# A Perceiver block's first cross-attention: the context's fp16 remainders made by GpSimd instead of VectorE

## The chip, the cores and the metric

The kernel runs on one core of a Trainium2 chip. The metric is the device time of one execution in microseconds (us); lower is better. The engines are named as the profile names them: PE is TensorE's matmul unit (PEld its weight load), DVE is VectorE, ACT is ScalarE, POOL is GpSimd and SP the engine that issues the DMAs.

## The reference

A block of six residual steps works on 128 latent rows of 256 channels. The first step, in which the change lies, is a cross-attention of 16 heads over a context of 12544 rows:

```python
xn = _layernorm(x, ln_gamma, ln_beta)
q = (xn @ w_q).reshape(B, SQ, NUM_HEADS, DIM_HEAD)      # 128 queries, 16 heads of 64
kv = context @ w_kv                                     # context 12544 x 256, w_kv 256 x 2048
k, v = jnp.split(kv, 2, axis=-1)
scores = jnp.einsum('bqhd,bkhd->bhqk', q * SCALE, k)
attn = jax.nn.softmax(scores, axis=-1)
out = jnp.einsum('bhqk,bkhd->bqhd', attn, v).reshape(B, SQ, INNER)
return (out @ w_out + b_out) * jnp.tanh(gate[0])
```

Then follow a causal attention, a feed-forward with quantised weights, a second cross-attention over the same context, a selective scan and a mixture of experts. All arithmetic is fp32 in the reference.

## The kernel before

`first_cross_attention` cuts the context into 14 chunks of 896 rows (`NCH = 14`, `CH = 896`, chunk `c`) and walks in each through the 16 heads `h`; one head of one chunk is a step, `n = 16 * c + h`, 224 steps in all. Every engine has its own program, written out by hand in Python loops over `n`; each executes its program strictly in order, and the engines are coupled by counting semaphores alone.

fp32 operands are split into two fp16 parts, a rounded one and a remainder, and three fp16 products stand in for one fp32 product. For the context this split is made once per chunk, one chunk ahead, in four pieces `k` of 128 x 448: ScalarE writes the rounded part `c_hi` (`c_high`, at its steps h = 5 to 8), VectorE the remainder `c_lo` = `c_raw` * `c_scale` - `c_hi` (`c_low`, one instruction per piece, at its steps h = 6 to 9). `c_raw` is the loaded fp32 chunk; it has one buffer, and `c_hi` and `c_lo` have two (`par`).

The parts of a step, by engine:

- TensorE, step n: `turn_max(n + 1)` (L793, by which the start of a step is seen), the key products of unit U = n + 6 (`k_wait(U)`, then `k_part`, L771, six products), `first_pass(n + 2)`, `lay_max(n + 1)` (L798), `weigh(n - 1)`, `second_pass(n + 1)`, and at 14 of the 16 steps (not at h = 0 and 8) six value products (`v_project`, L743). A unit U holds the keys of two heads for half a chunk, so the units 16(c+1) and 16(c+1)+1, made at h = 10 and h = 11, are the first that read the next chunk.
- ScalarE, step n: value rounding, `p_high(n)`, `m_row(n + 1)`, `k_copy(n + 6)` into `k_raw`, `exponent(n + 1)`, then `c_high` where it is due, and at every fourth step the `decay` of the running maximum.
- VectorE, step n: `new_max(n + 1)` (L601), `v_low` (or `c_low` of piece 3 at h = 9), `tiles_max(n + 2)` (L592), every fourth step `flush`, `p_low(n)` (`pT_lo`, L606), then `c_low` of pieces 0 to 2 at h = 6 to 8.
- GpSimd, step n: at h % 4 = 3 the scaling of the accumulator (`acc`, L421), which waits for ScalarE's `decay` of the same step; `k_split(n + 6)`, a cast `k_top` (L404) and a subtraction `k_rest` (L406) that split `k_raw`; at h % 4 = 2 `group_max` (L391 to L396).
- SP issues the DMAs that place `k_top` and `k_rest` in `k_st`, and at h = 11 the load of the next but one chunk into `c_raw`.

The waits of TensorE for the remainders are these (`c_lo_ready` counts finished pieces, four a chunk):

```python
if u < 2:                                   # k_wait(U), u = U % 16: first two units of a chunk
    pe.wait_ge(c_lo_ready, 4 * c + 2 + 2 * u)
if half == 0:                               # v_project, steps h = 9 to 15
    pe.wait_ge(c_lo_ready, 4 * c + (2 if tile < 3 else 4))
```

So pieces 0 and 1 of the next chunk are wanted at the end of TensorE's step h = 9, and all four at its step h = 11. ScalarE's `k_copy` waits until `k_rest` of two units earlier is done, since `k_raw` has two buffers.

Of the kernel before, what the change touches and what calls it, by code (L numbers as in the profile page):

```python
# [5 lines left out]
ALU = mybir.AluOpType  # L6
# [14 lines left out]
NCH = SK // CH  # L21
# [27 lines left out]
def at_least(engine, sem, value):  # L49

    if isinstance(value, int) and value <= 0:
        return
    engine.wait_ge(sem, value)
# [98 lines left out]
def first_cross_attention(nc, ctx, a, sb, sem, x, z, y, zT, ident, st, stats, rows, cols, gate, ps,  # L152
# [11 lines left out]
    with ExitStack() as own:  # L164
        def t(name, shape, dt=F32):
            return sb(name, shape, dt, own)
# [15 lines left out]
        c_raw = t("c_raw", [P, DC, CH])  # L182
        c_hi, c_lo = t("c_hi", [P, 2, DC, CH], F16), t("c_lo", [P, 2, DC, CH], F16)
        c_abs, c_scale = t("c_abs", [P, 2, 4]), t("c_scale", [P, 2, DC])
# [21 lines left out]
        def tf_half(w, j):  # L206
            return w[TERNARY[j // 2]][:, j % 2 * INNER:(j % 2 + 1) * INNER]
# [20 lines left out]
        c_hi_ready, c_lo_ready = sem("c_hi_ready"), sem("c_lo_ready")  # L228
# [41 lines left out]
        def v_at(n):  # L270

            c, h = n // H0, n % H0
            if 1 <= h <= TILES:
                return c * 14 + 6 + h, c, 1, h - 1
            if h >= 9 and c + 1 < NCH:
                return c * 14 + 5 + h, c + 1, 0, h - 9
            return None
# [10 lines left out]
        def raw_part(k):  # L288
            return (slice(None), k % 2, slice(k // 2 * HCH, (k // 2 + 1) * HCH))

        def c_part(par, k):
            return (slice(None), par, k % 2, slice(k // 2 * HCH, (k // 2 + 1) * HCH))

        with nc.Block() as block:
# [56 lines left out]
            def _(pool):  # L351
                link = plink.on(pool)
# [23 lines left out]
                def unscale(c):  # L376
                    par = c % 2
                    pool.wait_ge(un_ready, c + 1)
                    nc.gpsimd.tensor_scalar(v_unscale[:, par:par + 1], un[:, par:par + 1], 1.0 / W_TOP, None, ALU.mult).then_inc(unscale_ready, 1)
                    nc.gpsimd.tensor_scalar(esc[:, par:par + 1], un[:, par:par + 1], q_un[:, 0:1], DH ** -0.5 / (W_TOP * K_DOWN), ALU.mult, ALU.mult).then_inc(unscale_ready, 1)  # L380
                    pool.wait_ge(unscale_ready, 2 * c + 2)
                    pool.wait_ge(c_scale_ready, c + 1)
                    link(nc.gpsimd.tensor_scalar(m_per[:, par:par + 1], un_inv[:, par:par + 1], q_scale[:, 0:1], W_TOP * K_DOWN * DH ** 0.5, ALU.mult,
                                                 ALU.mult))

                def group_max(c, g):

                    par, hs = c % 2, slice(4 * g, 4 * g + 4)
                    at_least(pool, decay_ready, c * 4 + g - 3)
                    pool.wait_ge(m_ready, c * H0 + 4 * g + 4)  # L390
                    link(nc.gpsimd.tensor_scalar(run_max[:, par, hs], m_col[:, par, hs], esc[:, par:par + 1], None, ALU.mult))  # L391
                    nc.gpsimd.tensor_tensor(drop[:, hs], run_max[:, 1 - par, hs], run_max[:, par, hs], ALU.subtract).then_inc(drop_ready, 1)
                    f = c * 4 + g + 2
                    if 4 <= f < NCH * 4:
                        par, hs = f // 4 % 2, slice(4 * (f % 4), 4 * (f % 4) + 4)
                        nc.gpsimd.tensor_scalar(m_floor[:, hs], run_max[:, 1 - par, hs], m_per[:, par:par + 1], None, ALU.mult).then_inc(floor_ready, 1)  # L396

                def k_split(U):
                    i, b = U - K_AHEAD, U % 2

                    pool.wait_ge(k_raw_ready, i + 1)
                    if i >= 2:
                        pool.wait_ge(k_placed[b], k_turn(U - 2))
                    nc.gpsimd.tensor_copy(k_top[:, b, :], k_raw[:, b, :]).then_inc(k_top_ready, 1)  # L404
                    pool.wait_ge(k_top_ready, i + 1)
                    nc.gpsimd.tensor_tensor(k_rest[:, b, :], k_raw[:, b, :], k_top[:, b, :], ALU.subtract).then_inc(k_rest_ready, 1)  # L406
# [5 lines left out]
                for n in range(NT):  # L412
                    c, h = n // H0, n % H0
                    if h % 4 == 3:
                        g = h // 4
                        f = c * 4 + g

                        pool.wait_ge(decay_ready, f + 1)
                        at_least(pool, flushed, 2 * (f - 3))
                        grp = acc[:, 4 * g:4 * g + 4, :]  # L420
                        nc.gpsimd.tensor_tensor(grp, grp, decay[:, 4 * g:4 * g + 4].unsqueeze(2).to_broadcast([P, 4, DH + 1]),  # L421
                                                ALU.mult).then_inc(acc_scaled, 1)
                    if n + K_AHEAD < NT:
                        k_split(n + K_AHEAD)
                    if h == 5 and c + 1 < NCH:
                        unscale(c + 1)
                    if h % 4 == 2:
                        group_max(c, h // 4)

            @block.scalar  # L430
            def _(act):
# [124 lines left out]
            def _(v):  # L556
                link = vlink.on(v)
# [13 lines left out]
                def c_low(c, k):  # L571
                    par = c % 2
                    v.wait_ge(c_hi_ready, 4 * c + k + 1)
                    nc.vector.scalar_tensor_tensor(out=c_lo[c_part(par, k)], in0=c_raw[raw_part(k)], scalar=c_scale[:, par, k % 2:k % 2 + 1],
                                                   in1=c_hi[c_part(par, k)], op0=ALU.mult, op1=ALU.subtract).then_inc(c_lo_ready, 1)
# [19 lines left out]
                def new_max(n):  # L595
                    c, h, i = n // H0, n % H0, n % 2
                    m = m_col[:, c % 2, h:h + 1]
                    v.wait_ge(max_turned, n + 1)
                    if c > 0 and h % 4 == 0:
                        v.wait_ge(floor_ready, c * 4 + h // 4 - 3)  # L600
                    nc.vector.tensor_scalar(turned[:, i, :], s_turned(n), 1.0, -BIG if c == 0 else m_floor[:, h:h + 1], ALU.mult, ALU.max,  # L601
                                            accum_out=m).then_inc(m_ready, 1)
# [77 lines left out]
                for n in range(NT):  # L680
                    c, h = n // H0, n % H0
                    if n + 1 < NT:
                        new_max(n + 1)
                    if n and v_at(n - 1):
                        v_low(*v_at(n - 1))
                    elif c + 1 < NCH:
                        if h == 1:
                            absmax(c + 1, 2)
                        if h == 9:
                            c_low(c + 1, 3)  # L690
                    if n + 2 < NT:
                        tiles_max(n + 2)
                    if h % 4 == 1 and n > 1:
                        flush(n // 4 - 1)
                    p_low(n)
                    if h == 15 and c + 2 < NCH:
                        absmax(c + 2, 0)
                    if c + 1 < NCH:
                        if h in (0, 3):
                            absmax(c + 1, (1, 2, 0, 3)[h])  # L700
                        if h == 4:
                            scale(c + 1)
                        if 6 <= h <= 8:
                            c_low(c + 1, h - 6)
                    if c == 1 and h == 4:
                        v.wait_ge(tf_total, 1)
                        link(nc.vector.tensor_reduce(tf_mean[:, :], s_total.rearrange("p (k b) -> p k b", b=2), AX.X, ALU.add))
                        link(nc.vector.tensor_scalar(tf_mean[:, :], tf_mean[:, :], 1.0 / (D * INNER), 1e-5, ALU.mult, ALU.max))
                        nc.vector.reciprocal(tf_inv[:, :], tf_mean[:, :]).then_inc(tf_mean_ready, 1)
                    if 2 <= c < 8 and h == 13:  # L710
                        j = c - 2
                        v.wait_ge(tf_scaled, 2 * j + 2)
                        link(nc.vector.tensor_scalar(tf_half(tf_raw, j), tf_half(tf_raw, j), ROUND, 1.0, ALU.subtract, ALU.min))
                    if 2 <= c < 8 and h == 15:
                        j = c - 2
                        nc.vector.tensor_scalar(tf_half(tf_wq, j), tf_half(tf_raw, j), -1.0, None, ALU.max).then_inc(tf_quantised, 1)
# [1136 lines left out]
```

## Time and profile before

| | before |
| --- | --- |
| median of 3 runs | 1372.73 us |
| lowest, highest | 1368.29, 1372.86 us |
| profiled execution, its own time | 1368.9 us |
| its span, first to last instruction | 1367.2 us |
| PE busy | 1157.3 us (85%) |
| DVE busy | 1075.5 us (79%) |
| ACT busy | 857.6 us (63%) |
| POOL busy | 625.3 us (46%) |

The profile is one execution, followed by the hardware profiler. The busy shares are averages over all six residual steps; the first one fills the span from about 50 to about 970 us, and only it contains the instructions of the change. PE's spans are modelled, so its distance from full use is better read from the starts of its steps than from its busy share.

### The profile page before, as it was taken

To read this page: it belongs to the slowest core of one execution; us is meant where nothing else is said; L and a number is where in the kernel's file an instruction comes from. 1 tells how busy PE (TensorE), PEld (TensorE's weight loads), DVE (VectorE), ACT (ScalarE), POOL (GpSimd) and SP (SyncE) were. 2 spreads that over 40 slices of the span, in tenths; PEclk is the share of its full clock that TensorE was granted. 3 is DMA by queue.
4 is the path that set the end of the run, shared out by engine and by line. 5 is a ranking of instruction groups with operands and counts; after the bars stand their busy time and mean duration, and the time that the engine had idled before them with its cause. 6 is when DMAs were issued, how large, how long until landed. Compare 5 with 4: busy or idle time off the path is not lost. (4 is left out here: it accounts for less than half of the span.)

```text
span 1367.2 us, 31601 instructions
## 1 busy us (share of the span) xinstructions
PE 1157.3 (85%) x12091; PEld 794.4 (58%) x12091; DVE 1075.5 (79%) x1757; ACT 857.6 (63%) x1453; POOL 625.3 (46%) x734
## 2 busy tenths in 40 slices
PE   3699999999999999999999999999539895135598
PEld 1366666666666666666666666666415584012397
DVE  7678989898989899999898998988445414999522
ACT  2489888888888888888888888888310231550010
POOL 5056666565656666656666566665000000556000
PEclk9999999999999999999999999999858997576699
DMA  5154343434343434344443434334356370500165
GB/s 198 57 134 110 84 118 92 113 88 111 86 113 86 109 82 113 87 111 93 113 116 89 113 83 117 85 91 97 138 183 202 107 228 2 215 0 1 69 233 186
DMA packets 137137, 152.21 MB, mean 111 GB/s; under 512 B 17617, under 2 KB 125457, under 8 KB 136737
## 3 DMA queue, kind: packets, MB, share of 16 engines
q1 hardware_dynamic: 136176, 147.12, 39.7%
q10 hardware_dynamic: 816, 3.15, 0.6%
q8 instruction: 93, 1.52, 0.5%
q14 instruction: 52, 0.42, 0.1%
HBM read 74.34 MB, written 0.16 MB: 54 GB/s over the span
## 5 line engine op out<-in xcount | busy, mean ns | idle before, releaser
L406 POOL TENSOR_TENSOR k_rest<-k_raw,k_top 128x448 f16<-128x448 f32 x218 | 316.3, 1451 | 17.6
L476 ACT ACTIVATE p_exp<-ps,ln_k,esc 128x896 f32<-128x896 f32 x224 | 246.1, 1099 | 70.3 <-PE ps L807 65.5
L606 DVE TENSOR_TENSOR pT_lo<-p_exp,pT_hi 128x896 f16<-128x896 f32 x224 | 271.4, 1212 | 2.3 <-ACT pT_hi L494 2.3
L592 DVE TENSOR_REDUCE tile_max<-ps 128x128 f16<-128x896 f32 x224 | 243.3, 1086 | 33.4 <-PE ps L784 33.1
L404 POOL CAST k_top<-k_raw 128x448 f16<-128x448 f32 x218 | 143.2, 657 | 223.0 <-ACT k_raw L489 180.8
L494 ACT ACTIVATE pT_hi<-p_exp 128x896 f16<-128x896 f32 x224 | 211.3, 943 | 0.6
L587 DVE TENSOR_TENSOR v_lo<-ps,v_hi 128x512 f16<-128x512 f32 x196 | 135.1, 689 | 49.8 <-ACT v_hi L468 46.0
L821 PE MATMUL ps<-v_hi,pT_hi 128*128 128x65 f16 x1568 | 164.1, 193 | 2.5 <-DVE pT_lo L606 2.5
L822 PE MATMUL ps<-v_lo,pT_hi 128*128 128x64 f16 x1568 | 164.2, 193 | 0.0
L823 PE MATMUL ps<-v_hi,pT_lo 128*128 128x65 f16 x1568 | 163.8, 193 | 0.0
L771 PE MATMUL ps<-c_hi,wk_hi 128*128 128x448 f16 x448 | 158.3, 353 | 3.7 <-DVE k_st L658 3.6
L771 PE MATMUL ps<-c_hi,wk_lo 128*128 128x448 f16 x448 | 158.6, 354 | 0.0
L771 PE MATMUL ps<-c_lo,wk_hi 128*128 128x448 f16 x448 | 158.4, 354 | 0.0
L743 PE MATMUL ps<-wv_lo,c_hi 128*128 128x512 f16 x392 | 149.1, 380 | 0.0
L743 PE MATMUL ps<-wv_hi,c_lo 128*128 128x512 f16 x392 | 149.1, 380 | 0.0
L743 PE MATMUL ps<-wv_hi,c_hi 128*128 128x512 f16 x392 | 149.1, 380 | 0.0
L821 PEld LDWEIGHTS ps<-v_hi,pT_hi 128*128 128x128 f16 x1568 | 144.9, 98 | 2.8 <-DVE pT_lo L606 2.8
L823 PEld LDWEIGHTS ps<-v_hi,pT_lo 128*128 128x128 f16 x1568 | 142.9, 97 | 0.0
L822 PEld LDWEIGHTS ps<-v_lo,pT_hi 128*128 128x128 f16 x1568 | 142.8, 97 | 0.0
L784 PEld LDWEIGHTS ps<-q_hi,k_st 128*128 128x128 f16 x1568 | 105.8, 98 | 49.1 <-ACT p_exp L476 5.5
L468 ACT ACTIVATE v_hi<-ps 128x512 f16<-128x512 f32 x196 | 116.4, 594 | 26.3 <-PE ps L743 22.7
L784 PE MATMUL ps<-q_hi,k_st 128*128 128x128 f16 x1568 | 124.1, 219 | 7.8 <-ACT p_exp L476 3.0
(330 smaller groups left out, 2120.4 us busy)
## 6 DMA issues: line engine op xcount, KB each, us to landing
k_st<-k_top SPq DMA_DIRECT2D x436, 112.0 KB, 2.3
k_st<-k_rest SPq DMA_DIRECT2D x436, 56.0 KB, 2.0
c_raw<-in_ctxT SPq DMA_DIRECT2D x14, 896.0 KB, 5.9
xa_ct<-in_ctxT SPq DMA_DIRECT2D x14, 896.0 KB, 4.7
xa_cn<-in_ctx SPq DMA_DIRECT2D x14, 896.0 KB, 5.1
me_w<-in_me_w SPq DMA_DIRECT2D x8, 1536.0 KB, 7.8
me_w<-in_me_w SPq DMA_DIRECT2D x8, 768.0 KB, 4.8
ss_b_all<-ss_bc SPq DMA_DIRECT2D x1, 2048.0 KB, 6.7
```

The source lines that it names most:

```text
L404: nc.gpsimd.tensor_copy(k_top[:, b, :], k_raw[:, b, :]).then_inc(k_top_ready, 1)
L406: nc.gpsimd.tensor_tensor(k_rest[:, b, :], k_raw[:, b, :], k_top[:, b, :], ALU.subtract).then_inc(k_rest_ready, 1)
L476: nc.scalar.activation(p_exp[:, n % 2, :], s_scores[n % 2], ACT.Exp, bias=ln_k[:, 0:1], scale=esc[:, n // H0 % 2:n // H0 % 2 + 1]).then_in ...
L494: nc.scalar.activation(pT_hi[:, n % 2, :, :].rearrange("p t s -> p (t s)"), p_exp[:, n % 2, :], ACT.Copy).then_inc(pT_hi_ready, 1)
L592: nc.vector.tensor_reduce(tile_max[:, n % 2, :], s_scores[n % 2].rearrange("p (t s) -> p s t", s=S), AX.X, ALU.max).then_inc(tile_max_done, 1)
L606: nc.vector.tensor_tensor(pT_lo[:, n % 2, :, :].rearrange("p t s -> p (t s)"), p_exp[:, n % 2, :], pT_hi[:, n % 2, :, :].rearrange("p t s ...
L743: mm = nc.tensor.matmul(v_bank(vn), lhs, rhs, start=(k == 0), stop=(k == 5))
L771: mm = nc.tensor.matmul(k_bank(U), lhs, rhs, start=(k == 0), stop=(k == 5))
L784: mm = nc.tensor.matmul(s_scores[i][:, tile * S:(tile + 1) * S], k_st[:, n // 2 % 4, i, 0, tile * P:(tile + 1) * P], q_hi[:, h, :], start= ...
L821: nc.tensor.matmul(to, ph, v_hi[:, tile, h, 0:DH + 1], start=(tile == 0), stop=False)
L822: nc.tensor.matmul(to[:, 0:DH], ph, v_lo[:, tile, h, 0:DH], start=False, stop=False)
L823: mm = nc.tensor.matmul(to, pl, v_hi[:, tile, h, 0:DH + 1], start=False, stop=(tile == TILES - 1))
```

## The change

VectorE's `c_low` goes from its steps h = 6 to 9 (it stays for chunk 0, before the loop). GpSimd does the same pieces at its steps h = 6 to 9, behind `k_split` and `group_max` of the step. It has no single instruction for it there: it first scales a piece of `c_raw` in place and then subtracts `c_hi`, with a wait on its own semaphore between (`link`). TensorE's, ScalarE's and SP's programs are unchanged.

```diff
@@ gpsimd, at the end of step n
                     if h % 4 == 2:
                         group_max(c, h // 4)
+                    if 6 <= h <= 9 and c + 1 < NCH:
+                        k, par = h - 6, (c + 1) % 2
+                        pool.wait_ge(c_hi_ready, 4 * (c + 1) + k + 1)
+                        link(nc.gpsimd.tensor_scalar(c_raw[raw_part(k)], c_raw[raw_part(k)], c_scale[:, par, k % 2:k % 2 + 1], 1.0, ALU.mult, ALU.mult))
+                        nc.gpsimd.tensor_tensor(c_lo[c_part(par, k)], c_raw[raw_part(k)], c_hi[c_part(par, k)], ALU.subtract).then_inc(c_lo_ready, 1)
@@ vector, step n
                     elif c + 1 < NCH:
                         if h == 1:
                             absmax(c + 1, 2)
-                        if h == 9:
-                            c_low(c + 1, 3)
...
                         if h == 4:
                             scale(c + 1)
-                        if 6 <= h <= 8:
-                            c_low(c + 1, h - 6)
```

On GpSimd, from the accumulator's scaling (`acc`) of step h = 7 to the maximum (`run_max`) of h = 10, the order was this: four splits of the keys in a row (h = 7 to 10).

```order
L421 TENSOR_TENSOR acc<-acc,decay 128x260
L404 CAST k_top<-k_raw 128x448
L406 TENSOR_TENSOR k_rest<-k_raw,k_top 128x448
L404 CAST k_top<-k_raw 128x448
L406 TENSOR_TENSOR k_rest<-k_raw,k_top 128x448
L404 CAST k_top<-k_raw 128x448
L406 TENSOR_TENSOR k_rest<-k_raw,k_top 128x448
L404 CAST k_top<-k_raw 128x448
L406 TENSOR_TENSOR k_rest<-k_raw,k_top 128x448
L391 TENSOR_SCALAR run_max<-m_col,esc 128x4
```

In the changed kernel, in the same stretch from the row behind `acc` on, GpSimd's order is this (piece 0 stands ahead of `acc`, behind the `group_max` of h = 6).

```order
L404 CAST k_top<-k_raw 128x448
L406 TENSOR_TENSOR k_rest<-k_raw,k_top 128x448
L432 TENSOR_SCALAR c_raw<-c_raw,c_scale 128x448
L433 TENSOR_TENSOR c_lo<-c_raw,c_hi 128x448
L404 CAST k_top<-k_raw 128x448
L406 TENSOR_TENSOR k_rest<-k_raw,k_top 128x448
L432 TENSOR_SCALAR c_raw<-c_raw,c_scale 128x448
L433 TENSOR_TENSOR c_lo<-c_raw,c_hi 128x448
L404 CAST k_top<-k_raw 128x448
L406 TENSOR_TENSOR k_rest<-k_raw,k_top 128x448
L432 TENSOR_SCALAR c_raw<-c_raw,c_scale 128x448
L433 TENSOR_TENSOR c_lo<-c_raw,c_hi 128x448
```

Between `acc` and the last remainder of a chunk now stand three splits of the keys and three pairs of the new instructions, where the remainders took no place in this queue before.

On VectorE, from `pT_lo` of step h = 7 to `tile_max` of step h = 9, the order was this.

```order
L606 TENSOR_TENSOR pT_lo<-p_exp,pT_hi 128x896
L574 SCALAR_TENSOR_TENSOR c_lo<-c_raw,c_scale,c_hi 128x448
L601 TENSOR_SCALAR turned,m_col<-ps 128x128
L587 TENSOR_TENSOR v_lo<-ps,v_hi 128x8x64
L592 TENSOR_REDUCE tile_max<-ps 128x128
L606 TENSOR_TENSOR pT_lo<-p_exp,pT_hi 128x896
L574 SCALAR_TENSOR_TENSOR c_lo<-c_raw,c_scale,c_hi 128x448
L601 TENSOR_SCALAR turned,m_col<-ps 128x128
L574 SCALAR_TENSOR_TENSOR c_lo<-c_raw,c_scale,c_hi 128x448
L592 TENSOR_REDUCE tile_max<-ps 128x128
```

In the changed kernel the same stretch of VectorE's queue is this (its lines lie five further down).

```order
L611 TENSOR_TENSOR pT_lo<-p_exp,pT_hi 128x896
L606 TENSOR_SCALAR turned,m_col<-ps 128x128
L592 TENSOR_TENSOR v_lo<-ps,v_hi 128x8x64
L597 TENSOR_REDUCE tile_max<-ps 128x128
L611 TENSOR_TENSOR pT_lo<-p_exp,pT_hi 128x896
L606 TENSOR_SCALAR turned,m_col<-ps 128x128
L597 TENSOR_REDUCE tile_max<-ps 128x128
```

Nothing but `c_lo` is gone, so `turned` (`new_max`) stands directly behind `pT_lo`.

## Rows read from the trace of the kernel before

**Rows 1.** Busy time of PE, PEld, DVE, ACT, POOL; clock, DMA share, GB/s.

```profile
100.00:950.00 850.00, 826.16 (x10211) 561.72 (x10210) 768.56 (x1277) 715.06 (x1145) 523.76 (x665) 1.00 0.42 100
```

**Rows 2.** Timeline of PE, chunk 9, h = 7 to 12: start, duration, [idle before].

```profile
686.19 0.22 PE L793 MATMUL ps<-ident,tile_max 128*128 128x128 f16 x1
...
688.10 0.23 PE L798 MATMUL ps<-ident,m_col 128*128 128x128 f16 x1 [0.16 <-DVE turned L601]
...
690.47 0.22 PE L793 MATMUL ps<-ident,tile_max 128*128 128x128 f16 x1
...
693.40 0.23 PE L793 MATMUL ps<-ident,tile_max 128*128 128x128 f16 x1
...
695.63 0.23 PE L798 MATMUL ps<-ident,m_col 128*128 128x128 f16 x1 [0.47 <-DVE turned L601]
...
698.28 0.22 PE L793 MATMUL ps<-ident,tile_max 128*128 128x128 f16 x1
...
702.30 0.22 PE L793 MATMUL ps<-ident,tile_max 128*128 128x128 f16 x1
702.36 0.35 PE L771 MATMUL ps<-c_hi,wk_hi 128*128 128x448 f16 x1
...
706.25 0.22 PE L793 MATMUL ps<-ident,tile_max 128*128 128x128 f16 x1
```

**Rows 3.** Timeline of DVE, the same chunk: `pT_lo` and `c_lo`.

```profile
686.31 1.45 DVE L574 SCALAR_TENSOR_TENSOR c_lo<-c_raw,c_scale,c_hi 128x448 f16<-128x448 f32 x1
...
689.56 1.07 DVE L606 TENSOR_TENSOR pT_lo<-p_exp,pT_hi 128x896 f16<-128x896 f32 x1
690.56 0.67 DVE L574 SCALAR_TENSOR_TENSOR c_lo<-c_raw,c_scale,c_hi 128x448 f16<-128x448 f32 x1
...
693.26 1.14 DVE L606 TENSOR_TENSOR pT_lo<-p_exp,pT_hi 128x896 f16<-128x896 f32 x1
694.33 0.97 DVE L574 SCALAR_TENSOR_TENSOR c_lo<-c_raw,c_scale,c_hi 128x448 f16<-128x448 f32 x1
...
695.49 1.18 DVE L574 SCALAR_TENSOR_TENSOR c_lo<-c_raw,c_scale,c_hi 128x448 f16<-128x448 f32 x1
...
698.06 1.35 DVE L606 TENSOR_TENSOR pT_lo<-p_exp,pT_hi 128x896 f16<-128x896 f32 x1
...
701.21 1.24 DVE L606 TENSOR_TENSOR pT_lo<-p_exp,pT_hi 128x896 f16<-128x896 f32 x1
```

**Rows 4.** Timeline of POOL, the same chunk.

```profile
688.20 0.30 POOL L396 TENSOR_SCALAR m_floor<-run_max,m_per 128x4 f32<-128x4 f32 x1
691.21 0.62 POOL L421 TENSOR_TENSOR acc<-acc,decay 128x260 f32<-128x260 f32 x1 [2.71 <-ACT decay L534]
691.78 0.56 POOL L404 CAST k_top<-k_raw 128x448 f16<-128x448 f32 x1
692.42 1.04 POOL L406 TENSOR_TENSOR k_rest<-k_raw,k_top 128x448 f16<-128x448 f32 x1
693.40 1.42 POOL L404 CAST k_top<-k_raw 128x448 f16<-128x448 f32 x1
694.90 1.29 POOL L406 TENSOR_TENSOR k_rest<-k_raw,k_top 128x448 f16<-128x448 f32 x1
696.79 0.56 POOL L404 CAST k_top<-k_raw 128x448 f16<-128x448 f32 x1 [0.60 <-ACT k_raw L489]
...
701.58 1.76 POOL L406 TENSOR_TENSOR k_rest<-k_raw,k_top 128x448 f16<-128x448 f32 x1
```

**Rows 5.** Groups by line and shape: count | busy us, mean ns | idle.

```profile
L574 DVE SCALAR_TENSOR_TENSOR c_lo<-c_raw,c_scale,c_hi 128x448 f16<-128x448 f32 x51 | 54.3, 1064 | 0.0
...
L380 POOL TENSOR_SCALAR esc<-un,q_un 128x1 f32<-128x1 f32 x14 | 3.7, 267 | 1.3
...
L374 POOL CAST ident<-ident 128x128 f16<-128x128 f32 x1 | 0.3, 291 | 0.1
```

**Rows 6.** Timeline of ACT, the same chunk: `pT_hi` of h = 11.

```profile
703.00 0.94 ACT L494 ACTIVATE pT_hi<-p_exp 128x896 f16<-128x896 f32 x1
```

## The prediction

> **What bounds the kernel now.** I read first the busy time of the engines in the stretch from 100 to 950 us, which is inside the first cross-attention [rows 1]. PE is busy for 826.16 of 850 us at full clock, DVE for 768.56, ACT for 715.06, POOL for 523.76. So TensorE sets the pace, VectorE runs close behind it, and GpSimd seems to have room: 38% of its time is free.
>
> Then I read the starts of TensorE's steps in one chunk [rows 2]. A step starts at L793. The step h = 11, from 702.30 to 706.25, lasts 3.95 us and shows no wait, so I take 3.95 as TensorE's own time for a step with value products. The steps around VectorE's `c_low` are h = 7: 690.47 - 686.19 = 4.28; h = 8 (no value products): 693.40 - 690.47 = 2.93; h = 9: 698.28 - 693.40 = 4.88; h = 10: 702.30 - 698.28 = 4.02. Over 3.95 that is 0.33 at h = 7, 0.93 at h = 9 and 0.07 at h = 10; h = 8 can't be compared so; I give it 0.2. The bracketed waits of 0.16 and 0.47 us name `turned`, the instruction that stands behind `c_lo` on VectorE [rows 2, 3]. VectorE's remainders thus cost TensorE at most about 1.5 us a chunk, and that is the most the relief can bring: 13 x 1.5 = 20 us.
>
> Last I read GpSimd's own timeline in that chunk, because an average of 38% free says nothing about one queue at one place. Behind its `group_max` (688.20 + 0.30) it idles 2.71 us until `decay` of h = 7 is there and `acc` starts, at 691.21 [rows 4]. From there it has 11.15 us until TensorE starts the key products of h = 11 at 702.36 [rows 2], which in the changed kernel want all four pieces of `c_lo`.
>
> **How GpSimd and VectorE share time.** The cast `k_top` takes 0.56 us when nothing disturbs it, but 1.42 at 693.40, beside the `pT_lo` of 693.26 [rows 3, 4]: 0.86 more. The subtraction `k_rest` takes 1.04 at 692.42, but 1.76 at 701.58, beside the `pT_lo` of 701.21: 0.72 more. In reverse, `pT_lo` of 698.06 lasts 1.35 beside `k_rest`'s tail, against 1.07 at 689.56, and `c_lo` lasts 0.67 alone and up to 1.45. So the two engines exclude each other in these instructions, and each `pT_lo` takes about 0.86 us out of a busy GpSimd queue. (The Trainium skill, "SBUF — State Buffer", section "SBUF: two separate sides", calls the pair of ports an exclusive lock that the loser waits for; the trace's 0.86 agrees.)
>
> **The change part by part.**
>
> VectorE loses 4 instructions per chunk, 13 chunks, of 1064 ns on average [rows 5]. By the above that frees at most 1.5 us of TensorE's time a chunk.
>
> GpSimd gains 4 pairs a chunk. The subtraction has the shape and types of `k_rest`: from 692.42 to the next start at 693.40, 0.98 us. The in-place scaling (fp32 out, two multiplies, one by a value per partition) is in no row. From below it is bounded by the cast of the same size, 0.56; from above by the two-input subtraction, 1.04. Between them I build it from small rows: a scaling with two scalars on one column costs 0.267, and the cast of 128 columns 0.291 against 0.56 for 448, which is 0.84 ns a column; 0.267 + 447 x 0.00084 = 0.64 us [rows 4, 5]. With the 0.08 us that a wait on its own semaphore costs (691.78 + 0.56 to 692.42), the pair is 0.64 + 0.08 + 0.98 = 1.70 us. A split of the keys is 0.64 + 0.98 = 1.62.
>
> The Trainium skill speaks more strongly against the move: "GPSIMD Engine Reference", section 3, has a two-input elementwise operation 1.96 times as long on GpSimd as on VectorE. From c_lo's undisturbed 0.67 that would be a subtraction of 1.31 instead of 1.04 us; three of them would add 0.8 us a chunk, 11 us in all. The row of `k_rest` is the same operation on the same shape, so I keep 1.04.
>
> Piece 0 is free: it stands in the 2.71 us of idle before `acc`. It needs 1.70, and one `pT_lo` (689.56) falls into it, 0.86, in sum 2.56.
>
> From the start of `acc` to the end of piece 3 the queue now holds: `acc` 0.57, three splits 3 x 1.62 = 4.86, three pairs 3 x 1.70 = 5.10, and three `pT_lo` that cut in (those of h = 8, 9, 10; that of h = 11 can't start before its `pT_hi` ends at 703.94 [rows 6], and comes as late as TensorE does) 3 x 0.86 = 2.58. The sum is 13.11 us, and 0.1 for the signal. There is no gap to win back: `k_raw` is ready earlier than GpSimd comes to it (at 696.79 it had still waited 0.60 for it). TensorE would be ready after 11.15. **So it waits 13.2 - 11.15 = 2.1 us at `k_wait` of step h = 11, in each of 13 chunks: 27 us.** Behind that wait are `first_pass`, `lay_max`, `weigh` and `second_pass`, so ScalarE and VectorE stand still with it, and the whole pipeline shifts.
>
> What is given back: the relief of h = 8 to 10 is lost, since it only brings TensorE to the same wait sooner. Relief ahead of `acc` counts, because it starts the chain earlier: of h = 7's 0.33, the 0.16 that was a wait plus a little, say 0.2. And VectorE enters h = 11 without arrears, another 0.25. In sum 0.45 x 13 = 6 us.
>
> Other consumers have room. Pieces 0 and 1 are ready at 691.21 + 0.57 + 1.62 + 1.70 + 0.86 = 695.96; TensorE wants them in the last microsecond of h = 9, from about 697. `k_rest` of h = 9 ends near 701.8, ScalarE's copy that needs it free is that of h = 11. The placed keys are wanted three and more steps later. SP's load of `c_raw` stands behind `k_rest` of h = 11 in both kernels.
>
> The sum: 27 - 6 = +21 us. On the profiled execution's 1368.9 that is 1390; on the median of 1372.73, which is 3.8 above it, 1394. I say **1392 us**.
>
> **The rivals.**
>
> *A, the forecast: GpSimd's queue is late for h = 11, by 1 to 3 us.* 1380 to 1405. Chance 0.68.
>
> *B, GpSimd is much later.* If the scaling costs the upper bound, 1.04, each pair is 0.40 longer and the wait 3 x 0.40 = 1.2 longer: 13 x 1.2 = 16 us more, about 1408. If each `pT_lo` takes its full 1.07, 0.6 us a chunk more, 8 us. For it: no row has fp32 written by GpSimd at this width. Against it: the small scalings cost no more than the small cast. Chance 0.16.
>
> *C, faster: the remainders are in time.* This needs the chain to fit in 11.15 us: 10.53 of GpSimd's own work, so each `pT_lo` may take no more than 0.2 us from it. Then TensorE gets back its excess up to the moment when piece 3 is there, 702.36 - 701.9 = 0.5, with 0.45 from above about 0.9 us a chunk, 12 us: 1360. For it: the casts of 691.78 and 696.79 run undisturbed in 0.56 [rows 4], as if room could be found between VectorE's instructions. Against it: in a queue without idle each `pT_lo` must hold up one instruction or the next. Chance 0.07.
>
> *D, no change.* The wait is 0.3 to 0.7 us, as large as what is given back. This needs a `pT_lo` to cost about 0.4. 1366 to 1379. Chance 0.09.
>
> **How the numbers follow.** A measurement of this kernel tells 0.5%, 7 us, from no change. Slower by more: A and B, 0.84; within: D, 0.09; faster: C, 0.07. The range has the lower end from the short values (scaling 0.56, `pT_lo` 0.72 each: wait 1.4, less 0.45: 12 us, and somewhat more given back), and the upper from B: 1377 to 1410.
>
> **What would show it.** After the change TensorE's L771 at h = 11 should show a wait of about 2 us for GpSimd's `c_lo`, 13 times, some 25 us in all, and be the longest wait of TensorE in the stretch. VectorE's busy time in it should fall by about 50 us, with longer `pT_lo` at h = 7 to 10. GpSimd should run without idle from `acc` of h = 7 to piece 3, 13.1 us. The scaling should read 0.64 us undisturbed. The prediction is wrong if that wait is absent (then C or D), or if ScalarE waits for `k_rest` (then more is late than I see).

## The result: slower by 2.4%

The changed kernel takes 1403.79 us (median of 4 runs, 1402.34 to 1408.41), the kernel before 1372.8 us (4 runs). The ratio is 1.024, 95% interval 1.0207 to 1.0272: 31 us more. The forecast was 1392, with a range from 1377 to 1410: the direction and the place were right, the size was over a third too small (19 us forecast, 31 measured).

The page of the changed kernel, its first part and the groups that changed (lines lie one to five further down than before):

```profile
span 1400.6 us, 31653 instructions
...
PE 1164.9 (83%) x12091; PEld 803.1 (57%) x12091; DVE 1044.3 (75%) x1705; ACT 858.7 (61%) x1453; POOL 711.4 (51%) x838
...
L597 DVE TENSOR_REDUCE tile_max<-ps 128x128 f16<-128x896 f32 x224 | 243.9, 1089 | 78.9 <-PE ps L785 78.6
...
L772 PE MATMUL ps<-c_hi,wk_hi 128*128 128x448 f16 x448 | 159.9, 357 | 34.3 <-POOL c_lo L433 30.7
```

VectorE's busy time fell from 1075.5 to 1044.3 us: `c_lo` takes 55.7 us less, `pT_lo` 14.7 us more (from 271.4 to 286.1). What VectorE gained it spends waiting for TensorE (78.9 us of idle ahead of `tile_max`, where it was 33.4). The view of who waited for whom, for PE, from 100 to 970 us (waiter, releaser: us in total, times, longest):

```profile
PE ps L772 <- POOL c_lo L433: 30.7, 13, 2.5
PE ps L808 <- ACT q_low L488: 6.8, 20, 1.4
PE ps L799 <- DVE turned L606: 5.8, 18, 0.5
```

Thirteen waits, one for each chunk that has a successor, all at the key products and all for GpSimd's remainder. Twelve of them last 2.47 or 2.48 us; the one in the first chunk lasts 1.03. The wait for `turned` is down to 5.8 us in 18 times. In the kernel before, the same view had this, the part around `c_lo` included:

```profile
PE ps L798 <- DVE turned L601: 14.7, 44, 1.0
```

GpSimd's timeline in chunk 9 answers to [rows 4]:

```profile
707.50 0.30 POOL L396 TENSOR_SCALAR m_floor<-run_max,m_per 128x4 f32<-128x4 f32 x1
707.78 0.64 POOL L432 TENSOR_SCALAR c_raw<-c_raw,c_scale 128x448 f32<-128x448 f32 x1
708.50 1.04 POOL L433 TENSOR_TENSOR c_lo<-c_raw,c_hi 128x448 f16<-128x448 f32 x1
710.56 0.62 POOL L421 TENSOR_TENSOR acc<-acc,decay 128x260 f32<-128x260 f32 x1 [1.01 <-ACT decay L539]
711.12 0.56 POOL L404 CAST k_top<-k_raw 128x448 f16<-128x448 f32 x1
711.76 1.04 POOL L406 TENSOR_TENSOR k_rest<-k_raw,k_top 128x448 f16<-128x448 f32 x1
712.78 1.48 POOL L432 TENSOR_SCALAR c_raw<-c_raw,c_scale 128x448 f32<-128x448 f32 x1
714.34 1.04 POOL L433 TENSOR_TENSOR c_lo<-c_raw,c_hi 128x448 f16<-128x448 f32 x1
...
719.51 0.56 POOL L404 CAST k_top<-k_raw 128x448 f16<-128x448 f32 x1
720.14 1.84 POOL L406 TENSOR_TENSOR k_rest<-k_raw,k_top 128x448 f16<-128x448 f32 x1
721.97 0.64 POOL L432 TENSOR_SCALAR c_raw<-c_raw,c_scale 128x448 f32<-128x448 f32 x1
722.68 1.03 POOL L433 TENSOR_TENSOR c_lo<-c_raw,c_hi 128x448 f16<-128x448 f32 x1
```

And PE's, at its step h = 11 of the same chunk and the start of the next step:

```profile
721.17 0.22 PE L794 MATMUL ps<-ident,tile_max 128*128 128x128 f16 x1
...
723.86 0.35 PE L772 MATMUL ps<-c_hi,wk_hi 128*128 128x448 f16 x1 [2.47 <-POOL c_lo L433]
...
727.75 0.22 PE L794 MATMUL ps<-ident,tile_max 128*128 128x128 f16 x1
```

Piece 3 is finished at 723.71, 13.15 us behind the start of `acc`; between the two GpSimd has no bracket of idle. The scaling lasts 0.64 us undisturbed, and 1.48 at 712.78, 0.84 more, where VectorE is in this `pT_lo`:

```profile
712.61 1.14 DVE L611 TENSOR_TENSOR pT_lo<-p_exp,pT_hi 128x896 f16<-128x896 f32 x1
```

TensorE reaches step h = 11 at 721.17, 10.61 us behind `acc` and not 11.09, because the relief of h = 9 and 10 did come, and then it waits. Its step lasts 727.75 - 721.17 = 6.58 us instead of 3.95.

Something in the same place was not foreseen. In chunk 6 the products behind the wait are slow:

```profile
517.87 0.22 PE L794 MATMUL ps<-ident,tile_max 128*128 128x128 f16 x1
...
520.56 0.39 PE L772 MATMUL ps<-c_hi,wk_hi 128*128 128x448 f16 x1 [2.48 <-POOL c_lo L433]
520.75 0.57 PE L772 MATMUL ps<-c_lo,wk_hi 128*128 128x448 f16 x1
521.12 0.58 PE L772 MATMUL ps<-c_hi,wk_lo 128*128 128x448 f16 x1
...
526.10 0.22 PE L794 MATMUL ps<-ident,tile_max 128*128 128x128 f16 x1
```

and the granted clock of the stretch behind the wait, from 520.6 to 524.0 us, and of the next one is (PE, PEld, DVE, ACT, POOL busy; clock, DMA share, GB/s):

```profile
520.60:524.00 3.40, 3.40 (x24) 2.19 (x25) 0.40 (x1) 0.27 (x2) 2.10 (x5) 0.52 0.29 66
524.80:528.00 3.20, 3.20 (x33) 1.95 (x31) 2.06 (x5) 2.70 (x5) 1.64 (x3) 1.00 0.07 18
```

0.52 is the lower of the two levels, 1.2 instead of 2.4 GHz. This step lasts 526.10 - 517.87 = 8.23 us, 1.65 more than that of chunk 9. It happened behind 7 of the 12 waits of 2.47 us and not behind the one of 1.03 (the L772 products start 0.37 us apart there and 0.19 elsewhere); the seven steps last 8.05 to 8.24 us, 11.3 us in all over the 6.58 of the others; in the kernel before, the clock stands at 1.00 over the whole stretch [rows 1].

### The profile page after: what moved, and what is told of

Its sections match the earlier page's. It is cut to its first block and busy times, and to the rows that moved or that the text cites. A ratio compares the mean times of both kernels' runs of the same rounds, so it can differ in the third digit from the quotient of the medians.

```text
span 1400.6 us, 31653 instructions
## 1 busy us (share of the span) xinstructions
PE 1164.9 (83%) x12091; PEld 803.1 (57%) x12091; DVE 1044.3 (75%) x1705; ACT 858.7 (61%) x1453; POOL 711.4 (51%) x838
## 5 line engine op out<-in xcount | busy, mean ns | idle before, releaser
L406 POOL TENSOR_TENSOR k_rest<-k_raw,k_top 128x448 f16<-128x448 f32 x218 | 312.8, 1435 | 17.6
L597 DVE TENSOR_REDUCE tile_max<-ps 128x128 f16<-128x896 f32 x224 | 243.9, 1089 | 78.9 <-PE ps L785 78.6
L611 DVE TENSOR_TENSOR pT_lo<-p_exp,pT_hi 128x896 f16<-128x896 f32 x224 | 286.1, 1277 | 2.5 <-ACT pT_hi L499 2.5
L404 POOL CAST k_top<-k_raw 128x448 f16<-128x448 f32 x218 | 130.6, 599 | 182.3 <-ACT k_raw L494 142.1
L772 PE MATMUL ps<-c_hi,wk_hi 128*128 128x448 f16 x448 | 159.9, 357 | 34.3 <-POOL c_lo L433 30.7
L822 PE MATMUL ps<-v_hi,pT_hi 128*128 128x65 f16 x1568 | 167.3, 194 | 2.5 <-DVE pT_lo L611 2.5
L823 PE MATMUL ps<-v_lo,pT_hi 128*128 128x64 f16 x1568 | 167.3, 194 | 0.0
L824 PE MATMUL ps<-v_hi,pT_lo 128*128 128x65 f16 x1568 | 166.7, 194 | 0.0
L772 PE MATMUL ps<-c_hi,wk_lo 128*128 128x448 f16 x448 | 160.8, 359 | 0.0
L772 PE MATMUL ps<-c_lo,wk_hi 128*128 128x448 f16 x448 | 160.7, 359 | 0.0
L808 PE MATMUL ps<-q_low,k_st 128*128 128x128 f16 x1568 | 125.3, 220 | 9.3 <-ACT q_low L488 9.1
```

What stands on the lines that cost most here:

```text
L597: nc.vector.tensor_reduce(tile_max[:, n % 2, :], s_scores[n % 2].rearrange("p (t s) -> p s t", s=S), AX.X, ALU.max).then_inc(tile_max_done, 1)
L611: nc.vector.tensor_tensor(pT_lo[:, n % 2, :, :].rearrange("p t s -> p (t s)"), p_exp[:, n % 2, :], pT_hi[:, n % 2, :, :].rearrange("p t s ...
L772: mm = nc.tensor.matmul(k_bank(U), lhs, rhs, start=(k == 0), stop=(k == 5))
L822: nc.tensor.matmul(to, ph, v_hi[:, tile, h, 0:DH + 1], start=(tile == 0), stop=False)
L823: nc.tensor.matmul(to[:, 0:DH], ph, v_lo[:, tile, h, 0:DH], start=False, stop=False)
L824: mm = nc.tensor.matmul(to, pl, v_hi[:, tile, h, 0:DH + 1], start=False, stop=(tile == TILES - 1))
```

## The experiments

Eight kernels ran, in two groups of four; their times stand against the kernel before in the same group (1372.82 us, then 1371.01 us).

**Does the clock account for the rest?** `warm` is the changed kernel; TensorE does ten products that nobody reads, into the bank that the real ones then overwrite, before it waits.

```diff
+                    if u == 1 and c > 0:
+                        for k in range(10):
+                            nc.tensor.matmul(k_bank(U), wk_hi[:, 0, 0:P], c_hi[:, 1 - c % 2, 0, 0:HCH], start=True, stop=True)
                     if u < 2:
                         pe.wait_ge(c_lo_ready, 4 * c + 2 + 2 * u)
```

> TensorE does ten throwaway key products (128x448, overwritten by the real ones) at h = 11 before it waits for the remainders, so it works through most of the 2.5 us wait. Clock theory: 7 of the 13 waits of the changed kernel are followed by 3.4 us at the lower clock, 1.6 us lost each, 11 us in all; with TensorE kept busy the clock stays up, L772 products behind the wait take 0.35 us and never 0.57, and the time falls from 1404 to about 1393. Rival: the extra behind the wait is the pipeline's latency when it resumes; then the time stays at 1404 though the clock stays up.

It takes 1391.46 us (1390.24 to 1393.25), 1.0142 of the kernel before (1.0117 to 1.0167), and 12.3 us less than the changed kernel, by doing more work. PE at h = 11 of chunk 9, where the ten products fill the wait and nothing behind them is slow:

```profile
715.57 0.22 PE L797 MATMUL ps<-ident,tile_max 128*128 128x128 f16 x1
715.63 2.05 PE L764 MATMUL ps<-c_hi,wk_hi 128*128 128x448 f16 x10
718.17 0.36 PE L775 MATMUL ps<-c_hi,wk_hi 128*128 128x448 f16 x1 [0.49 <-POOL c_lo L433]
718.37 0.35 PE L775 MATMUL ps<-c_lo,wk_hi 128*128 128x448 f16 x1
...
722.07 0.22 PE L797 MATMUL ps<-ident,tile_max 128*128 128x128 f16 x1
```

The step lasts 6.50 us here and 6.50 or 6.51 in eleven other chunks; piece 3 is ready as late as before (13.16 us behind `acc`), and the granted clock shows 1.00 from 100 to 970 us. Only in the first chunk, where the wait was short, do the ten products make the step longer (5.84 instead of 5.14 us). The rival is refuted: the time did not stay at 1404, and a step behind a wait of 2.47 us at full clock was 6.58, hardly more than here. So about 12 of the 31 us are the clock (11.3 by the seven steps), and 1391.46 - 1372.82 = 18.6 us are the wait less the relief.

**Does GpSimd's order set the wait?** `swap` lets the pair of a step stand ahead of its key split.

```diff
+                    if 6 <= h <= 9 and c + 1 < NCH:
+                        ... the pair of piece h - 6
                     if n + K_AHEAD < NT:
                         k_split(n + K_AHEAD)
                     if h == 5 and c + 1 < NCH:
                         unscale(c + 1)
                     if h % 4 == 2:
                         group_max(c, h // 4)
-                    if 6 <= h <= 9 and c + 1 < NCH:
-                        ... the pair of piece h - 6
```

> GpSimd does the pair of a step ahead of the key split and not behind it. Queue theory: only two splits (2 x 1.62) and three pairs (3 x 1.70) stand between acc and piece 3, so it is ready 10.6 to 11.5 us behind the start of acc instead of 13.3, TensorE comes at 10.6, waits 0 to 0.9 us, and the clock stays up; 1361 to 1374 us. Rival: GpSimd is simply overloaded and the splits, now late, hold up ScalarE's k_copy or the placing; then the time stays near 1400 with a wait of ScalarE for k_rest.

1377.71 us, ratio 1.0034 (1.0018 to 1.005): 26 us are won back, but 5 stay; the time is 4 us above the upper end expected. Piece 3 is ready 10.8 to 11.6 us behind `acc`, as expected. The waits of PE and ACT from 100 to 950 us:

```profile
PE ps L808 <- ACT q_low L488: 9.7, 27, 1.4
PE ps L772 <- POOL c_lo L427: 6.3, 8, 0.8
```

```profile
ACT decay L539 <- POOL drop L392: 10.0, 14, 1.4
ACT k_raw L494 <- POOL k_rest L406: 3.0, 9, 0.4
```

TensorE's wait for the remainders is down from 30.7 to 6.3 us, and the clock stays up. What is new is that ScalarE waits for GpSimd: 10.0 us for `drop`, in 12 of the 14 cases that of h = 6, ahead of which the pair and the split of its step now stand, and 3.0 for `k_rest`, as the rival said in its milder half. In neither of the two orders tried do the four pairs fit into GpSimd's queue at these steps without making someone wait.

**Which term of the sum?** `no_scale` leaves out the scaling of `c_raw` on GpSimd, so that the subtraction works on unscaled values and the remainders are wrong numbers.

```diff
-                        link(nc.gpsimd.tensor_scalar(c_raw[raw_part(k)], c_raw[raw_part(k)], c_scale[:, par, k % 2:k % 2 + 1], 1.0, ALU.mult, ALU.mult))
                         nc.gpsimd.tensor_tensor(c_lo[c_part(par, k)], c_raw[raw_part(k)], c_hi[c_part(par, k)], ALU.subtract).then_inc(c_lo_ready, 1)
```

> Leaves out the in-place scaling on GpSimd in the changed kernel (the context's remainders are then wrong numbers). Queue theory: three scalings with their waits, 3 x 0.72 = 2.2 us, go from the chain behind acc, piece 3 is ready at about 11.1 instead of 13.3, TensorE comes at 10.6 and waits 0.5 us, too short for the clock: 1372.8 - 0.9 x 13 + 0.5 x 13 = 1367 to 1370 us. Rival: the lock and not the sum of instructions decides; then a part of the 31 us stays, 1385 or more.

1363.46 us, ratio 0.9933 (0.9907 to 0.9958). PE has no wait for `c_lo` left at all. This is 4 us below the expected 1367 to 1370: piece 3 is ready 10.15 us behind `acc` and not 11.1, since with the shorter queue one `pT_lo` fewer falls into it. What then shows is the relief of VectorE alone: a period of a chunk is 0.9 us shorter, as expected, and 40 us lie between this and the changed kernel. It does not decide against the lock: the 3.0 us by which the chain is shorter are three scalings with their waits, 2.16, and one `pT_lo`, 0.84.

**And the ports?** `short_before` and `short_after` are the two kernels with a `pT_lo` of 128 of its 896 columns from the third step on; the other columns keep old values, so part of the attention's low product is stale.

```diff
-                    nc.vector.tensor_tensor(pT_lo[:, n % 2, :, :]..., p_exp[:, n % 2, :], pT_hi[:, n % 2, :, :]..., ALU.subtract)
+                    full = n < 2
+                    nc.vector.tensor_tensor(pT_lo[:, n % 2, 0:TILES if full else 1, :]..., p_exp[:, n % 2, 0:CH if full else S],
+                                            pT_hi[:, n % 2, 0:TILES if full else 1, :]..., ALU.subtract)
```

> The kernel before with pT_lo computed for 128 of its 896 columns from the third step on (the rest stays stale). It is the base for short_after. VectorE gets 0.8 us a step shorter, so TensorE's arrears to it fall: 1340 to 1365 us; k_rest should take 1.04 to 1.2 us on average instead of 1.45.

> The changed kernel with the same short pT_lo. Lock theory: each pT_lo now takes 0.1 to 0.2 us from GpSimd and not 0.86, so piece 3 is ready 10.9 to 11.2 us behind acc, TensorE waits 0.3 to 0.6 us without a clock loss: 0 to 8 us above short_before. Rival, GpSimd's own instructions make it late whatever VectorE does: piece 3 stays at 13 us and the difference is 20 to 31 us as in the full pair.

1349.6 us (1348.57 to 1350.94) and 1350.23 us (1349.01 to 1350.93): no difference that these runs can tell, where the full pair differs by 31 us. `k_rest` takes 1075 ns on average in `short_before`, where it took 1451 with the full `pT_lo`, as expected. GpSimd in `short_after`, chunk 9, from `acc` on:

```profile
677.11 0.62 POOL L421 TENSOR_TENSOR acc<-acc,decay 128x260 f32<-128x260 f32 x1 [1.72 <-ACT decay L539]
677.67 0.56 POOL L404 CAST k_top<-k_raw 128x448 f16<-128x448 f32 x1
678.31 1.04 POOL L406 TENSOR_TENSOR k_rest<-k_raw,k_top 128x448 f16<-128x448 f32 x1
679.33 0.67 POOL L432 TENSOR_SCALAR c_raw<-c_raw,c_scale 128x448 f32<-128x448 f32 x1
...
686.83 1.04 POOL L433 TENSOR_TENSOR c_lo<-c_raw,c_hi 128x448 f16<-128x448 f32 x1
```

Piece 3 is ready 687.87 - 677.11 = 10.76 us behind `acc`, against 13.15: the same instructions, 2.4 us shorter, which is 0.8 for each of three `pT_lo`. The lock theory stands. The rival, GpSimd's own instructions alone, would have left it at 13. There is no gain to be seen either: in `short_before` TensorE's steps h = 7 and 10 are already down to 3.95 us, so the move has nothing left to relieve.

**What is the relief worth, and what does it take?** Three kernels give GpSimd a part of the pieces. The finished pieces are counted by one semaphore, and TensorE takes a count of two for pieces 0 and 1; so an engine waits for the other's earlier piece where the count would otherwise be wrong.

```diff
 g02, GpSimd, behind group_max
+                    if h in (6, 8) and c + 1 < NCH:
+                        ... the pair of piece h - 6, behind a wait for c_lo_ready >= 4 * (c + 1) + h - 6
 g02, VectorE
-                        if 6 <= h <= 8:
-                            c_low(c + 1, h - 6)
+                        if h == 7:
+                            v.wait_ge(c_lo_ready, 4 * (c + 1) + 1)
+                            c_low(c + 1, 1)
                         if h == 9:
+                            v.wait_ge(c_lo_ready, 4 * (c + 1) + 2)
                             c_low(c + 1, 3)
```

> GpSimd does pieces 0 and 2, VectorE 1 and 3. Queue theory: piece 2 is ready 7.2 us behind the start of acc, TensorE never waits for it; VectorE's relief at h = 7 (0.34 us a chunk) and part of that at h = 9 (0.2 to 0.4) stay: 1363 to 1368 us, faster than both kernels. Rival: the relief of VectorE is worth nothing, 1373.

`g0` does piece 0 on GpSimd and the other three on VectorE.

```diff
+                    if h == 6 and c + 1 < NCH:
+                        ... the pair of piece 0 on GpSimd; c_low of 1, 2 and 3 stays at h = 7, 8 and 9
```

> GpSimd does piece 0 alone, in the 2.7 us that it idles before acc. Queue theory: nothing on GpSimd is late; the gain is that of h = 7, 0.34 us x 13 = 4 us: 1368 us. Rival: the lock against pT_lo of h = 7 (1.83 us instead of 1.08) eats it: 1373.

`g03` does pieces 0 (h = 6) and 3 (h = 8) on GpSimd, 1 and 2 on VectorE.

```diff
+                    if h in (6, 8) and c + 1 < NCH:
+                        ... the pair of piece 0 or 3 on GpSimd; c_low of 1 and 2 stays at h = 7 and 8
```

> GpSimd does pieces 0 and 3 (at h = 6 and h = 8), VectorE 1 and 2; no remainder stands before tile_max of h = 9, where flush already stands on VectorE. Queue theory: ready 7 to 8 us behind acc, no wait; the whole excess of h = 9 is gone if it came from piece 3 on VectorE: 1360 to 1364. Rival: piece 2 on VectorE at h = 8 delays turned as before (0.47 us), so the time is that of the split into 0 and 2 or above: 1364 to 1370.

| kernel | on GpSimd | us, median | ratio to before (95%) |
| --- | --- | --- | --- |
| g0 | 0 | 1373.3 | 0.9999 (0.9985 to 1.0013) |
| g03 | 0, 3 | 1368.59 | 0.9981 (0.9965 to 0.9997) |
| g02 | 0, 2 | 1363.92 | 0.9918 (0.9893 to 0.9943) |
| changed kernel | 0, 1, 2, 3 | 1403.79 | 1.024 (1.0207 to 1.0272) |

`g02` beats both kernels. `g0` missed: the 4 us of h = 7 were expected and nothing came. Where each gains and loses is seen from TensorE's steps in chunk 9, in us from one start of a step to the next:

| kernel | h = 7 | h = 8 | h = 9 | h = 10 | sum |
| --- | --- | --- | --- | --- | --- |
| before | 4.28 | 2.93 | 4.88 | 4.02 | 16.11 |
| g0 | 3.95 | 3.19 | 4.99 | 4.02 | 16.15 |
| g03 | 3.95 | 3.18 | 4.76 | 3.95 | 15.84 |
| g02 | 3.94 | 3.19 | 4.23 | 3.95 | 15.31 |
| no_scale | 3.94 | 2.94 | 4.46 | 3.96 | 15.30 |
| changed kernel | 3.95 | 2.93 | 4.47 | 3.95 | 15.30 |

`g0` does gain at h = 7 and loses it at h = 8 and 9. Its own rival is the reason. GpSimd's pair and VectorE's queue in `g0`, chunk 9:

```profile
692.37 1.03 POOL L433 TENSOR_TENSOR c_lo<-c_raw,c_hi 128x448 f16<-128x448 f32 x1
694.41 1.01 POOL L421 TENSOR_TENSOR acc<-acc,decay 128x260 f32<-128x260 f32 x1 [1.01 <-ACT decay L539]
```

```profile
692.52 1.83 DVE L611 TENSOR_TENSOR pT_lo<-p_exp,pT_hi 128x896 f16<-128x896 f32 x1
694.27 0.67 DVE L579 SCALAR_TENSOR_TENSOR c_lo<-c_raw,c_scale,c_hi 128x448 f16<-128x448 f32 x1
694.87 0.34 DVE L606 TENSOR_SCALAR_CACHE_REDUCE turned<-ps,m_floor 128x128 f16<-128x128 f32 x1
```

`pT_lo` waits for GpSimd's subtraction (1.83 us instead of 1.07), piece 1 and `turned` come that much later, and the pieces 2 and 3 behind them pass it on. `g02` suffers the same at h = 7 (its h = 8 is as long), but with piece 2 gone VectorE is level again by h = 9, and the sum is that of the kernels with no remainder on VectorE. In `g03` it is not, since piece 2 on VectorE stands ahead of `turned` at h = 8; there the rival was right and the hope for h = 9 wrong.

In `g02` GpSimd needs no more than this behind `acc`. Piece 2 ends at 695.79, 7.9 us after 687.85 (7.2 were expected; its subtraction lasts 1.76 instead of 1.04 us) and 2.7 before TensorE's step h = 11:

```profile
687.85 1.00 POOL L421 TENSOR_TENSOR acc<-acc,decay 128x260 f32<-128x260 f32 x1 [1.02 <-ACT decay L540]
...
693.31 0.64 POOL L433 TENSOR_SCALAR c_raw<-c_raw,c_scale 128x448 f32<-128x448 f32 x1
694.03 1.76 POOL L434 TENSOR_TENSOR c_lo<-c_raw,c_hi 128x448 f16<-128x448 f32 x1
```

## Why the prediction was right, and where it was short

**The place: right.** TensorE waits at `k_wait` of h = 11 for piece 3, 13 times, and it is the largest of its waits in the stretch. ScalarE has no wait for `k_rest` there, the sign that would have spoken against the forecast.

**The sum of the chain: right.** 13.11 us were summed, 13.15 measured. The scaling, priced from small rows at 0.64, is 0.64; the subtraction 1.03 to 1.04 as `k_rest`; a `pT_lo` costs 0.84 (1.48 - 0.64) and 0.80 by `short_after`, against 0.86. The price by the Trainium skill's ratio of 1.96 ("GPSIMD Engine Reference", section 3), 1.31 us for the subtraction, is not borne out: the trace has 1.03 to 1.04 for it.

**Piece 0 is free: right on GpSimd, wrong on VectorE.** It fits ahead of `acc` (1.01 us of idle remain), but its subtraction delays `pT_lo` of h = 7 by 0.76 us (1.83 at 692.52 in `g0`, 1.07 before). In the changed kernel this costs TensorE nothing (its h = 8 lasts 2.93 us as before), and no `c_lo` stands behind it on VectorE; in `g0` it takes back the whole gain.

**The wait less what is given back: nearly right as a difference, with both terms too small.** The text had 2.1 - 0.45 = 1.65 us a chunk, 21 us; `warm`, in which the clock plays no part, has 18.6 us, 1.43 a chunk. The waits are longer, 2.47 us in twelve chunks, because TensorE arrives 0.48 us earlier (10.61 instead of 11.09 behind `acc`); the text had said that this relief is lost, and it is.

**The most the relief can bring: too high.** The text took 3.95 us as TensorE's own time at h = 9 as well, gave h = 8 a relief of 0.2, and came to at most 1.5 us a chunk. With no remainder on VectorE h = 9 still takes 4.47 us and h = 8 takes 2.93 as before. The relief is 16.11 - 15.30 = 0.81 us in chunk 9. That agrees with the 0.9 that the text used for rival C.

**What was missing: the clock.** The step that failed is "so it waits 2.1 us in each of 13 chunks: 27 us". It priced the wait alone, as if TensorE resumed at full speed. Behind 7 of the 13 waits it resumed at half, 1.5 to 1.7 us each, 11 to 12 us in all, which `warm` gives back by idling less. With it the forecast's 21 would have been 33, where 31 were measured. Why it happened behind 7 of the 12 waits of 2.47 us and not behind the other 5, these runs don't show. That 1403.79 still lies in the 1380 to 1405 of forecast A is in part luck: that band allowed for a wait of up to 3 us, and what filled it was the clock.

**Outside the chunk loop** little moved. The first cross-attention ends, by ScalarE's read of the gate,

```profile
997.76 0.19 ACT L555 ACTIVATE tg<-gate 128x1 f32<-128x1 f32 x1
```

at 997.76 us; in the kernel before this was 967.93. Of the 33.4 us by which the two profiled spans differ 29.8 lie ahead of it, and 3.6 in the later stages, which share no instruction with the change; two executions of one kernel differ by as much.

**The rivals.** B, a dearer scaling, and the full 1.07 of a `pT_lo`, are refuted by the rows. C and D needed a `pT_lo` that takes 0.2 or 0.4 us from GpSimd's queue, and it takes 0.8. C's mechanism was sound and only its condition not met: with a `pT_lo` made short, `short_after` has the remainders nearly in time (its step h = 11 lasts 4.18 us in chunk 9 instead of 3.95), and where they are in time beside the full `pT_lo`, in `no_scale` and `g02`, the chunk does get shorter by about the 0.9 us that C gave it.

## What to carry to other kernels

An engine that is idle for a third of the time can still be the wrong place: add up its queue between the instruction that last released it and the consumer that waits, with the neighbour's instructions that lock the shared ports in the sum, and move only as much as fits. Of the splits tried here the best was two pieces of four, 0.8% faster, where four made it 2.4% slower; and it matters which two (`g03`, also with two, gained 0.2%). And the price of a new wait on TensorE can be the wait plus the clock behind it: a few throwaway products took 12 of 31 us away.

## What was not expected of the hardware

- Waits of 2.47 us, one in about 67 us, were enough for the granted clock to fall to 1.2 GHz for about 3.4 us (0.52 from 520.6 to 524.0), behind 7 of 12 of them. With 2.05 us of the wait filled by products it did not fall once, nor from 100 to 950 us in `swap`, where the longest wait of that kind was 0.8 us.
- GpSimd's scaling in place with an fp32 result, two multiplies and a per-partition scalar takes 0.64 us for 128 x 448 (707.78 and 721.97), hardly more than its cast to fp16 (0.56 at 711.12).
- Where `pT_lo` and an instruction of GpSimd's meet, the second to come is longer by about the rest of the first, on either side: 1.48 instead of 0.64 us for the scaling at 712.78, with 0.97 of `pT_lo` left; and 1.93 instead of 1.08 for the `pT_lo` at 716.00, which came in a `k_rest`:

```profile
716.00 1.93 DVE L611 TENSOR_TENSOR pT_lo<-p_exp,pT_hi 128x896 f16<-128x896 f32 x1
...
720.01 1.08 DVE L611 TENSOR_TENSOR pT_lo<-p_exp,pT_hi 128x896 f16<-128x896 f32 x1
```
